# TensorE's written-out stack padded to 1,024 instructions a step

## What is computed

```python
x = x + attn(_layernorm(x), Wq, Wk, Wv, Wo)           # 16 heads of 8, causal, over 256 tokens
x = x + stack(_layernorm(x), Wqkv, q_scale, k_scale, Wo, ln_g, ln_b, W1, b1, W2, b2)

# stack: six layers
for i in range(6):
    x = attn_layer(shift_tokens(x), Wqkv[i], q_scale[i], k_scale[i], Wo[i]) + x   # 16 heads of 64, windows of 32
    x = ffn_layer(shift_tokens(x), ln_g[i], ln_b[i], W1[i], b1[i], W2[i], b2[i]) + x
```

## The kernel before

| place | work | line |
|---|---|---|
| 0 to 48 | turn of x, projections V, Q, K, turns of q and xn | L1288, L1319, L1350, L1295 |
| 49 to 304 | `scores(n-1, 0)`, 128 pairs | L1363 |
| 305 to 369 | hidden layer, turns, two projections | L1311, L1350, L1319 |
| 370 to 671 | `values` four times (64 instructions each), `feed_out`, projections, a turn | L1334, L1373, L1319 |
| 672 to 928 | `scores(n-1, 1)`, 128 pairs | L1363 |
| 929 to 993 | `output` | L1341 |
| 994 to 1,020 | projection V, three turns | L1319, L1350 |

## Time and profile before

### The profile page before, as it was taken

One profiled execution on the slowest core, in us unless ns is written; L12 is line 12 of the kernel. 1 busy time (PEld: TensorE's weight loads), 2 busy tenths in 40 slices (PEclk: granted clock), 3 DMA queues, 4 the chain that ended last, 5 costly groups with the idle time before them and its releaser, 6 DMA issues.

```text
span 3346.3 us, 128353 instructions
## 1 busy us (share of the span) xinstructions
PE 3189.6 (95%) x51488; PEld 2280.0 (68%) x51488; DVE 2888.9 (86%) x5656; ACT 2792.8 (83%) x5313; POOL 2681.3 (80%) x1798
## 2 busy tenths in 40 slices
PE   8999799999999999999999999999999999999996
PEld 5777466776666666666666767777776776666665
DVE  6999788988888888888888889999999998888884
ACT  5776588888888888887888899988999998888884
POOL 1000498999989889988988999999999998898992
PEclk9999999999999999999999999999999999999998
DMA  2000011111211111211111211112211112111112
GB/s 68 0 0 0 1 39 35 35 37 47 59 38 36 40 40 49 51 40 33 34 40 49 51 40 40 40 36 56 49 40 40 40 40 55 44 40 29 38 40 53
DMA packets 127300, 128.92 MB, mean 39 GB/s; under 512 B 62380, under 2 KB 75824, under 8 KB 126832
## 3 DMA queue, kind: packets, MB, share of 16 engines
q1 hardware_dynamic: 123232, 112.38, 13.8%
q10 hardware_dynamic: 3600, 9.50, 0.9%
HBM read 19.04 MB, written 2.10 MB: 6 GB/s over the span
## 4 chain that ended last, share of the span: by engine, by line
PE 88%; issue 4%; DVE 3%; POOL 2%; ACT 1%; DMA 1%; SPq 1%; ACTq 0%; POOLq 0%; DVEq 0%
PE ps L1319 27%; PE ps L1341 11%; PE ps L1334 9%; PE ps L1350 9%; PE ps L1363 8%; PE ps L1311 8%; PE ps L1373 4%; PE ps L1175 3%; PE ps L1167 2%; PE ps L1164 2%; PE ps L1187 1%; PE ps L1160 1%; PE ps L1200 1%; POOL area L452 1%; PE ps L1295 1%
## 5 line engine op out<-in xcount | busy, mean ns | idle before, releaser
L1319 PE MATMUL ps<-Wqkv,xsT 128*128 128x512 f32 x2304 | 1108.0, 603 | 9.0 <-DMA Wqkv<-ffn_Wqkv 3.3
L452 POOL TENSOR_TENSOR area<-area,tab 128x512 f32<-128x512 f32 x768 | 958.3, 1276 | 38.3 <-ACT area L640 37.7
L1319 PEld LDWEIGHTS ps<-Wqkv,xsT 128*128 128x128 f32 x2304 | 392.7, 191 | 312.4 <-issue 201.2
L474 POOL TENSOR_TENSOR area<-area,lsum 128x1024 f32<-128x1024 f32 x192 | 365.4, 1903 | 281.5 <-DVE lsum L938 280.0
L640 ACT ACTIVATE area<-ps 128x512 f32<-128x512 f32 x768 | 455.1, 593 | 33.7 <-PE ps L1319 33.0
L459 POOL TENSOR_TENSOR area<-area 128x1024 f32<-128x1024 f32 x192 | 451.4, 2373 | 5.9 <-DVE area L997 5.5
L459 POOL TENSOR_TENSOR AQb<-AQb,area 128x1024 f32<-128x1024 f32 x192 | 449.8, 2365 | 0.1
L645 ACT ACTIVATE area<-area 128x1024 f32<-128x1024 f32 x384 | 396.5, 1065 | 0.1
L1341 PE MATMUL ps<-Wo,area 128*128 128x128 f32 x3072 | 377.0, 281 | 10.5 <-issue 10.4
L1363 PE MATMUL ps<-kT,area 64*32 64x64 f32 x24576 | 315.1, 225 | 59.8 <-issue 59.2
L1341 PEld LDWEIGHTS ps<-Wo,area 128*128 128x128 f32 x3072 | 357.4, 195 | 20.6 <-issue 11.9
(11 more groups left out here) (124 smaller groups left out, 6559.6 us busy)
## 6 DMA issues: line engine op xcount, KB each, us to landing
BD<-area SPq DMA_DIRECT2D x1440, 64.0 KB, 2.0
Wqkv<-ffn_Wqkv ACTq DMA_DIRECT2D x12, 512.0 KB, 4.4
x2s<-x2s SPq DMA_DIRECT2D x96, 56.0 KB, 2.1
Wo<-ffn_Wo SPq DMA_DIRECT2D x6, 512.0 KB, 5.1
Wqkv<-ffn_Wqkv ACTq DMA_DIRECT2D x12, 256.0 KB, 3.1
W<-ffn_W SPq DMA_DIRECT2D x6, 341.0 KB
x2s<-x2s SPq DMA_DIRECT2D x96, 7.5 KB, 2.1
x2s<-x2s SPq DMA_DIRECT2D x96, 0.2 KB, 1.7
```

What stands on the lines that cost most here:

```text
L452: pool.tensor_tensor(b4[:, :, here], q4[:, :, there], s4[:, :, here], ALU.mult).then_inc((s_bq, s_bk)[j], 1)
L474: pool.tensor_tensor(p3, p3, lsum[:, 1, :].unsqueeze(2).broadcast_to([P, HEADS, 2 * WIN]), ALU.mult).then_inc(s_pn, 1)
L1319: mm(home(kind + part), xsT[:, par, t * P:(t + 1) * P], Wqkv[:, w0:w0 + 512], start=True, stop=True).then_inc(done, 1)
```

## The change

A helper puts plain increments of a new semaphore `i_fill`, for which nobody waits, into TensorE's program. Ahead of step 0 there are 81 of them, and ahead of each step from 5 on two or three, so that each step from 5 to 95 takes up 1,024 instructions. The other engines' programs are unchanged, and so are the order and the number of TensorE's loads and matmuls. The built program has 346 more instructions on TensorE, all of them increments: 100,252.

```diff
+def fill(eng, counted, count):
+
+    for _ in range(count):
+        eng.sem_inc(counted, 1)
...
-                 "s_tab s_ct s_nq s_nk s_n0 s_half d_wv1 d_bd0 d_bd1")
+                 "s_tab s_ct s_nq s_nk s_n0 s_half d_wv1 d_bd0 d_bd1 i_fill")
...
                 if begin:
+                    fill(pe, i_fill, 81)
                     pe.wait_ge(a_oe, SEQS)
+                elif n > STATIC:
+                    fill(pe, i_fill, 2 if (n - 1) % SEQS in (0, 1, 3) else 3)
                 if now:
                     turn_x(n)
```

More of the change, by code:

```diff
@@ L154, in build @@
          s_o, s_oe, s_ve, s_wo, s_r1, d_sh, s_lnc, s_lnr, s_lnn, s_ln, s_xn, s_xne, s_h, s_gl, s_g, s_y, s_xc,
-         s_tab, s_ct, s_nq, s_nk, s_n0, s_half, d_wv1, d_bd0, d_bd1) = [S[n] for n in names.split()]
+         s_tab, s_ct, s_nq, s_nk, s_n0, s_half, d_wv1, d_bd0, d_bd1, i_fill) = [S[n] for n in names.split()]
         cosp = ps[:, 2, 0:SEQ].rearrange("p (t j d) -> p t j d", t=TILES, j=2)
```

## The result

| | before | after |
|---|---|---|
| median | 3324.64 us (4 runs) | 3474.2 us (4 runs, 3464.66 to 3475.4) |
| ratio | | 1.0431, 95% interval 1.039 to 1.0473 |
| profiled execution, its own time | 3348.17 us | 3475.40 us |
| its span | 3346.3 us | 3473.6 us |

The ratio is taken over all the runs of both kernels; the quotient of the two medians is 1.045. The forecast was 3240 us, 3210 to 3282. The time came out on the other side of the kernel before, and nearest to rival (b), 3435 us, which had 4%.

A forecast was written before the change was run, and what follows sets the result against it. The prediction took TensorE, stalled by late instruction packets, as the bound. Removing 102 us of gaps and adding 8 us for increments gave 3229 to 3254 us by median; it took 3240 us, range 3210 to 3282.

The forecast's parts named there:

- rival (b): New grid lies off the predicted place, every step bad at layer 2's 31.35 us: 3435 us, 3.4% slower; chance 4%.
- What bounds the kernel: TensorE, 95% busy, runs dry at 256-instruction edges when packets come late, costing up to 2 us a step in some layers.
- Where the edges would be: In steps 4 to 95, edges at 224, 480, 736 and 992 from the first load of `turn_x`.
- the good places: Edge places without gaps, modulo 256 within a step: 175 (layer 3's start) to 262 (layer 4's end), around step 66's 224.
- What the increments cost: Two or three a step on TensorE: bounded by 0 and 0.2 us a step, taken as 0.04 us, 4 us in all.
- rival (c): Increments are dear: all 346 paid at 0.15 us cost 52 us instead of 8, giving 3284 us; chance 8%.
- The 81: Increments ahead of step 0 delay the turn of x by about 2.5 to 10 us; taken as 4 us.
- What was to be removed: Gaps in steps 0 to 15, layers 1, 2, 3 and 5, and the drain: 102 us in all.
- the 24.7 us: Profiled execution's excess over the median run; even or all in gaps, giving 3229 or 3254 us; 3240 taken between.
- the lower bound of 3222: Low end of the forecast's own bounds: whole 102 us gone, fill hidden, 2.5 us for the 81 increments.
- The rule that spoke against it: Trainium skill's statement that crossing an instruction block boundary costs "one DMA tail-bump, mostly hidden", which would make the edges innocent.
- Rival (a): Edges are innocent and layers differ for another reason; nothing won, 8 us added: 3331 us, 0.24% slower; chance 3%.

The follow-up runs named there:

- e9: e5 with 97 increments in step 0 instead of 81, so edges stand at 208, 464, 720 and 976: 3253.6 us, ratio 0.9735.
- e2: Changed kernel with each step's two or three increments moved from the step's start to ahead of the first scores' waits: 3270.1 us, ratio 0.9798.
- e6: Changed kernel with each step's two or three increments some eight instructions earlier, ahead of the turn k00 and its wait: 3273.5 us.
- e11: Kernel before with one increment ahead of the turn of x in each of layer 4's 16 steps, nothing else: 3363.5 us.
- e4: Changed kernel with 113 increments ahead of step 0 instead of 81, edges at 192, 448, 704 and 960: 3336.7 us.
- e8: Changed kernel with one increment left at the start of each step from 5 on, the other one or two ahead of the first scores: 3525.1 us.
- e5: e2 with the 81 increments moved in step 0 to ahead of the turn k01, where TensorE waits anyway: 3261.5 us, ratio 0.977.
- e7: Changed kernel with each step's two or three increments right behind the turn of x instead of ahead of it: 3441.6 us.
- e12: Kernel before with the first transpose of the turn of x issued twice in layer 4's steps, no increments: 3323.9 us.
- e3: Changed kernel with 337 increments ahead of step 0 instead of 81: 3515.5 us.

## Why the prediction was wrong, point by point

**What bounds the kernel: right.** The gaps are missing instruction packets. In e9, where they are gone, layers 1 to 4 take 468.7 to 470.5 us.

**Where the edges would be: right.** 224 in each step, 88 pairs into the first scores.

**The step that failed** is "the good places reach from there 49 instructions down (to 175, where layer 3 begins) and 38 up", and with it "The forecast therefore goes by places that the run has tried". I took the goodness of an edge as a property of its place in the step. It depends on a second condition too: no semaphore instruction of its own between the wait of the step's last turn, k00, and the next step's first projections. The change puts its increments just there. In the kernel before this condition held in the steps of layer 4 but one, and that one, step 65, was a sign that I overlooked: its packet left 6.5 us after the step's start, where those of steps 64 and 66 left 0.3 us before it. e2 and e6 have the same edges with the increments elsewhere and lie at 3270 and 3273 us; e11 keeps the edges of layer 4 within the good range of before, adds one increment a step, and has a gap in 16 of 16 steps. Nor is the instruction enough without the place: with the edge at 192 (e4) or 208 (the second steps of e9) the packet left 2.7 to 5.7 us after the step's start, in time; with the edge at 219 to 246 it left 6.4 us after it or later.

**What the increments cost: wrong in kind.** I bounded them by their own time beside PE's work, 0 to 0.2 us a step, and allowed for more only as more of the same, 0.15 us for each in rival (c). As time they are indeed hidden in a step: e2's layer 4 has them and takes 469.2 us against 468.4. What they cost is the late packet, 1.9 us a step on average and sometimes a slower clock, and e8 shows that this has nothing to do with how long they last. My upper bound rested on the four semaphore instructions of the earlier trace rows, which stand at another place (ahead of the values) and so could not bound this.

**The 81: mis-sized.** I took 4 us of 2.5 to 10, and it came out above both: step 0 starts 11 us later. The rows of the increments in the changed kernel, those at the start and those at the end of step 70:

```profile
L46 PEldq EVENT_SEMAPHORE  x81: 51/51/51, 368.7 to 381.1; - x81
```

```profile
L46 PEldq EVENT_SEMAPHORE  x3: 51/51/51, 2612.1 to 2612.4; - x3
```

Each lasts 51 ns, but they follow each other 0.155 us apart (12.4 us over 80 steps). The turn of x waited 11.7 us. The duration in the record is not the rate.

**What was to be removed: about right.** I had 102 us. e2's median is 68 us below the kernel before on its chip; with the 11.7 us of the start and five gaps of some 2 us that remain, this is about 90. e9, whose 97 increments stand where PE waits anyway (that wait grew from 11.4 to 12.8 us; it was not the 19 us that I expected for e5), is 88.6 us below. The step that split the 24.7 us between the profiled run and the median had little to stand on: later runs of the kernel before took 3332 to 3354 us, so such differences are its ordinary spread. A slip with no weight here: the lower bound of 3222 adds up to 3224 by its own terms.

**The rule that spoke against it.** Crossing an edge is "mostly hidden", says the Trainium skill ("Runtime: NRT & Kernel Launch", instruction fetch mechanics). In e9, with 4 edges a step and no gap, it is hidden; in the changed kernel one edge of four stops PE for 1.5 to 2.5 us in each step from 5 to 94. Rival (a), which rested on it, is refuted by e9.

**The rivals.** Rival (b) had the right picture, a gap at one place in every step, and nearly the right price: it assumed 31.35 us a step and 31.6 were measured from step 5 to 94. Its reason, a shift of the grid, was not the one, so that its price came near is partly luck. Rival (c), increments dear in themselves, holds for the 81 alone.

**What stays open.** The runs show where a semaphore instruction costs the packet, not how the packet is asked for. In the good kernels the packet leaves from 0.4 us before to 1.1 us after the step's start, but for the second steps of layers; in the changed kernel it leaves only in the scores, 7.4 to 8.5 us after it, and in e4 from 2.7 us on. Why an edge at 9 to 48 misses it in layer 5 of before, without any increment, and why e4's edge at 960 finds a second moment, I can't say. That the increments break a run in which the sequencer would go on without a stop is a reading that fits e6, e7, e8, e11, e12 and the second steps of layers; it was not seen directly.

## What to carry to other kernels

In a long written-out program, look at "issue" gaps that creep from step to step: here they were instruction packets that came late, and padding the steps to a multiple of the packet let me choose where the edges lie, for 2.65% in the best version. Place the padding by trial: the same two or three increments gave 3270 us in the middle of a step and 3474 us behind the step's last wait. When a trace shows that some cases are good, ask what else those cases share before you build the forecast on the one thing you counted, and look at the odd one among them (here step 65).

## What the runs showed of the hardware

TensorE's instructions came in packets of 16,384 bytes, 256 instructions (390 packets in 6.39 MB), and a late one stopped the array for 1.5 to 2.8 us in the changed kernel and e8 though no semaphore was awaited. One plain increment between the wait of k00 and the turn of x made the packet leave some 7 to 8 us later with the edge at 219 to 246 (e11), while a weight load and a matmul more in the turn of x did not (e12). Plain increments in a row were 0.155 us apart at 51 ns each, and 0.154 us each over 256 of them in e3. Steps with such a gap also lost clock at times: step 70 of the changed kernel took 32.7 us at a granted clock of 0.95 and step 71 30.9 us at 1.00. The granted clock of its layers is 0.98 to 0.99, where e9, without gaps, has 1.00.

```profile
2579.80:2612.50 32.70, 30.91 (x502) 22.08 (x501) 26.82 (x52) 26.57 (x50) 27.35 (x18) 0.95 0.14 34
2612.50:2643.40 30.90, 29.27 (x503) 20.95 (x502) 27.07 (x52) 26.54 (x50) 27.38 (x18) 1.00 0.15 36
```
